# Earlier x loads in the prefix stages, and buffers of their own for two weight quarters in the second main super-tile

## The reference

```
xn  = layernorm(x)
q, k = xn @ Wq, xn @ Wk            # 1024 each, 4 heads of 256
v, gate = xn @ Wv, silu(xn @ Wg)   # 2048 each, 4 heads of 512
g   = log_sigmoid(xn @ Wgk1 @ Wgk2 + b) / 16
attn = gated linear attention over chunks, with a state S per head:
       S <- S * exp(sum g) + k^T v;  o = q S + masked (q k^T) v, rms-normed, * gate, @ Wo
ffn = top-2 of 4 experts, each  ln(relu(ln(xn @ W1 + b1)) @ W2 + b2), weighted
out = x + attn + ffn
```

## Time and profile before

| | us |
|---|---|
| timed runs, lowest, median, highest of 3 | 2788.45, 2792.22, 2792.83 |
| profiled execution, its own time | 2793.73 |
| its span, core 7 (slowest) | 2792.2 |
| its span, core 5 (fastest) | 2761.0 |
| busy on core 7: TensorE, VectorE, ScalarE | 1547.4, 951.5, 881.1 |

### The profile page before, as it was taken

How to read it: one execution, slowest core, us unless ns; L and a number is a source line. 1 busy time by engine, 2 the same in 40 slices (tenths; PEclk the granted TensorE clock), 3 DMA queues, 4 the chain that set the end, 5 groups by cost and what they waited for, 6 DMA issues and landing times.

```text
span 2792.2 us, 25322 instructions; the slowest of 8 cores (2761.0 to 2792.2 us)
## 1 busy us (share of the span) xinstructions
PE 1547.4 (55%) x6272; PEld 584.9 (21%) x6272; DVE 951.5 (34%) x2139; ACT 881.1 (32%) x1617; POOL 107.0 (4%) x152
## 2 busy tenths in 40 slices
PE   1390529235589055648766661289345656966850
PEld 0140104101234021213222220134112212322310
DVE  2432433243401233242255252520233322253253
ACT  2410632044223223214543433303322222533531
POOL 1000000000000000000010000000000000000000
PEclk9695769666799578768888875699767877988975
DMA  8022432162153300117363553035411004635323
GB/s 125 0 31 45 61 46 31 27 95 32 15 76 61 60 16 17 22 19 112 66 109 65 87 81 120 0 44 80 76 21 23 15 16 68 99 65 86 57 35 120
DMA packets 258284, 155.31 MB, mean 56 GB/s; under 512 B 173016, under 2 KB 242648, under 8 KB 258144
## 3 DMA queue, kind: packets, MB, share of 16 engines
q0 software_dynamic: 84576, 94.96, 22.5%
q1 hardware_dynamic: 168960, 41.96, 8.5%
q10 hardware_dynamic: 4608, 16.78, 1.8%
HBM read 198.04 MB, written 8.39 MB: 74 GB/s over the span
## 4 chain that ended last, share of the span: by engine, by line
PE 49%; DVE 19%; DMA 12%; issue 8%; ACT 7%; DVEq 2%; SPq 1%; ACTq 0%; POOL 0%; POOLq 0%
PE pa L287 20%; PE pb L287 19%; PE pf L287 7%; DVE s_bb L540 4%; DMA s_kgT<-s_kgs 4%; DVE s_kgs L653 2%; DMA s_gx<-x_tm 2%; DMA s_ogf<-s_ogc 2%; ACT s_sg L466 2%; DVEq L64 2%; PE pc L287 1%; PE pd L287 1%; DVE s_z L911 1%; DVE s_z L917 1%; DMA s_xt<-xp_tm 1%
## 5 line engine op out<-in xcount | busy, mean ns | idle before, releaser
L287 PE MATMUL pa<-s_w,s_xn 128*128 128x512 bf16 x1280 | 331.4, 406 | 350.7 <-DVE s_v L627 187.8
L287 PE MATMUL pb<-s_w,s_xn 128*128 128x512 bf16 x1280 | 310.0, 386 | 4.1 <-DMA s_w<-W 4.1
L287 PEld LDWEIGHTS pa<-s_w,s_xn 128*128 128x128 bf16 x1280 | 124.9, 102 | 521.9 <-issue 401.8
L287 PE MATMUL pf<-s_w,s_ogf 128*128 128x512 bf16 x512 | 150.7, 467 | 123.4 <-DMA s_ogf<-s_ogc 123.4
L287 PE MATMUL pa<-s_w,s_hfm 128*128 128x512 bf16 x512 | 128.2, 395 | 74.3 <-DMA s_hfm<-s_h 64.4
L750 ACT ACTIVATE s_jb<-s_ogc 128x512 bf16<-128x512 bf16 x64 | 40.3, 630 | 401.0 <-DVE s_ogc L744 399.0
L287 PEld LDWEIGHTS pb<-s_w,s_xn 128*128 128x128 bf16 x1280 | 122.2, 99 | 163.3 <-issue 33.5
L540 DVE TENSOR_TENSOR_SCAN s_bb<-c_os,s_bb 128x128 f32<-128x128 f32 x256 | 108.8, 425 | 106.1 <-ACT s_bb L533 80.2
L831 DVE TENSOR_TENSOR s_mcol<-s_scol 128x8 f32<-128x8 f32 x16 | 2.7, 167 | 400.9 <-ACT s_jb L891 400.3
L653 DVE TENSOR_SCALAR s_kgs<-s_kd,s_eb 128x128 bf16<-128x128 bf16 x256 | 65.3, 255 | 169.3 <-DMA s_kgT<-s_kgs 110.7
L287 PE MATMUL pb<-s_w,s_hfm 128*128 128x512 bf16 x512 | 122.4, 382 | 0.0
(11 more groups left out here) (176 smaller groups left out, 2278.3 us busy)
## 6 DMA issues: line engine op xcount, KB each, us to landing
s_w<-W POOLq DMA_DIRECT2D x32, 1024.0 KB, 13.5
s_w<-Wv_p POOLq DMA_DIRECT2D x8, 1024.0 KB, 19.2
s_w<-Wv POOLq DMA_DIRECT2D x8, 1024.0 KB, 10.7
s_w<-Wg POOLq DMA_DIRECT2D x8, 1024.0 KB, 17.5
s_w<-Wo POOLq DMA_DIRECT2D x8, 1024.0 KB, 12.0
s_gx<-x_tm ACTq DMA_DIRECT2D x16, 512.0 KB, 4.1
out<-s_jf ACTq DMA_DIRECT2D x16, 512.0 KB, 2.9
s_xt<-xp_tm POOLq DMA_DIRECT2D x4, 1024.0 KB, 10.5
```

The costliest lines, as they stand in the source:

```text
L287: ret = e.matmul(out=o, lhsT=l, rhs=r, start=st, stop=sp)
```

## The change

There are three parts. First, `stage_A_blk` takes two lists of waits in place of one: `load_w` for the x load and `sq_w` for the first Square, which writes `s_xntm`. In the prefix, the load is given no wait but for the x load before it, and the Square waits for all VectorE steps of stage C. The side task passes its list as `load_w`.

Second, two new buffers, `s_w4` at the place of `s_qg` and `s_w5` at that of `s_kd`, 1 MB each. After phase 5 of the first main super-tile's FFN, behind the transposes into `s_xn`, they are loaded with the first quarters of Wv and Wg. The load of `s_w4` waits for all steps of VectorE, ScalarE and TensorE so far; that of `s_w5` for the transposes (`tg`) and TensorE.

Third, the second main super-tile takes no slots for these two quarters; `proj_tm` reads them from the new buffers (`ded`). The slots in the rotation shift by two. The first Silu that writes `s_silu` now also waits for `g_marks`, the end of the output stage before it. The first main super-tile works as before, with slots.

```
...
     s_xntm = alloc("s_xntm", [128, 2, 4, D], BF16, at=offs["s_kd"])
+    s_w4 = alloc("s_w4", [128, NDC, 512], BF16, at=offs["s_qg"])
+    s_w5 = alloc("s_w5", [128, NDC, 512], BF16, at=offs["s_kd"])
...
-    def stage_A_blk(x_src, t0, blk, cpar, ext_w):
+    def stage_A_blk(x_src, t0, blk, cpar, load_w, sq_w=()):
...
-        g_dma(bsl[:, :, :], _rearr(rows), wait=[(gx, gx.n)] + list(ext_w), sem=gx)
+        g_dma(bsl[:, :, :], _rearr(rows), wait=[(gx, gx.n)] + list(load_w), sem=gx)
...
                 wait=[(gx, gw), (gd, cm)] +
-                     (([(tg[par], tg[par].n)] + list(ext_w)) if i == 0 else []))
+                     (([(tg[par], tg[par].n)] + list(sq_w)) if i == 0 else []))
...
-    def proj_tm(dst, Wd, act, vm, pre_slot=None, ev_w=()):
+    def proj_tm(dst, Wd, act, vm, pre_slot=None, ev_w=(), ded=None):
...
-            slot = pre_slot if (q4 == 0 and pre_slot is not None) \
-                else wu_next(Wd[:, q4 * 512:(q4 + 1) * 512])
-            gw = gsl[slot].n
+            if q4 == 0 and ded is not None:
+                wview, gwait = ded
+                slot = None
+            else:
+                slot = pre_slot if (q4 == 0 and pre_slot is not None) \
+                    else wu_next(Wd[:, q4 * 512:(q4 + 1) * 512])
+                wview = slotv(slot, NDC, 512)
+                gwait = (gsl[slot], gsl[slot].n)
...
                     s_op(lambda e, ps=ps, tc=tc, q4=q4: e.activation(
                         out=dst[:, tc, q4 * 512:(q4 + 1) * 512], in_=ps[:, :],
-                        func=act), wait=[(te, te.n)])
+                        func=act), wait=[(te, te.n)] + evw)
+                    evw = []
...
-        demark = [(te, te.n), (ve, ve.n)]
+        sqw = [(ve, ve.n)]
...
-        blks = [stage_A_blk(nsrc, nt0, b, ncp, demark) for b in range(NBLK)]
+        blks = [stage_A_blk(nsrc, nt0, b, ncp, (), sq_w=sqw)
+                for b in range(NBLK)]
...
-        pv = wu_next(Wv[:, 0:512])
-        pg2 = wu_next(Wg[:, 0:512])
+        if wu_pref[0] is not None:
+            dedv = wu_pref[0]
+            wu_pref[0] = None
+            pv = pg2 = None
+        else:
+            dedv = (None, None)
+            pv = wu_next(Wv[:, 0:512])
+            pg2 = wu_next(Wg[:, 0:512])
...
                 elif pi == 5:
                     xnm_n[0] = stage_A_xpose(nA[:NBLK], (te, te.n))
+                    g_dma(s_w4[:, :, :], _rearr(Wv[:, 0:512]),
+                          wait=[(ve, ve.n), (sc, sc.n), (te, te.n)], sem=gs4)
+                    g_dma(s_w5[:, :, :], _rearr(Wg[:, 0:512]),
+                          wait=[(tg[0], tg[0].n), (tg[1], tg[1].n),
+                                (te, te.n)], sem=gs5)
+                    wu_pref[0] = ((s_w4, (gs4, gs4.n)),
+                                  (s_w5, (gs5, gs5.n)))
...
```

More of the change, by code:

```diff
@@ L255, in build @@
     pl = mksem("pl")
+    gs4 = mksem("gs4")
+    gs5 = mksem("gs5")
     xd = mksem("xd")
@@ L407, in stage_A_xpose, with stage_A @@
         return xnm
-    def stage_A(x_src, t0, cpar, ext_w=()):
-        blks = [stage_A_blk(x_src, t0, blk, cpar, ext_w) for blk in range(NBLK)]
+    def stage_A(x_src, t0, cpar):
+        blks = [stage_A_blk(x_src, t0, blk, cpar, ()) for blk in range(NBLK)]
         return stage_A_xpose(blks, None)
@@ L619, in proj_tm @@
                     mm(ps[:, :], s_xn[:, dc, tc * 128:(tc + 1) * 128],
-                       slotv(slot, NDC, 512)[:, dc, :],
+                       wview[:, dc, :],
                        start=(dc == 0), stop=(dc == NDC - 1),
-                       wait=(w0 + [(gsl[slot], gw)] +
+                       wait=(w0 + [gwait] +
                              ([vm] if first else [])) if dc == 0 else [],
@@ L633, in proj_tm, with stage_C @@
                         out=dst[:, tc, q4 * 512:(q4 + 1) * 512], in_=ps[:, :],
-                        func=act), wait=[(te, te.n)])
+                        func=act), wait=[(te, te.n)] + evw)
+                    evw = []
                     rot.done(sc)
-            wu_done(slot)
-    def stage_C(prefix, eq_marks, em_marks, pre=(None, None)):
+            if slot is not None:
+                wu_done(slot)
+    def stage_C(prefix, eq_marks, em_marks, pre=(None, None),
+                ded=(None, None)):
         vm = (te, te.n)
-        proj_tm(s_v, Wv_p if prefix else Wv, None, vm, pre_slot=pre[0])
+        proj_tm(s_v, Wv_p if prefix else Wv, None, vm, pre_slot=pre[0],
+                ded=ded[0])
         if not prefix:
             proj_tm(s_silu, Wg, ACT.Silu, vm, pre_slot=pre[1],
-                    ev_w=g_marks[0])
+                    ev_w=g_marks[0], ded=ded[1])
         qbm = None
@@ L1143, in build @@
         eqm, emm = r_
-        tpms, qbm_, kbm_ = stage_C(False, eqm, emm, pre=(pv, pg2))
+        tpms, qbm_, kbm_ = stage_C(False, eqm, emm, pre=(pv, pg2), ded=dedv)
         if stop == "C" and st >= stop_st:
```

## The result

The changed kernel takes 2763.7 us, the median of 10 runs, against 2791.46 us for the kernel before, also 10 runs. The ratio is 0.9881, with a 95% interval of 0.9849 to 0.9912, so it is 1.2% faster. The prediction said 2764 us, range 2751 to 2778, and faster with a chance of 0.95. Runs in which one die had a lower clock than the other are left out of every ratio here; that is why a ratio can differ a little from the quotient of the medians. By the ratio the change saves 33 us, by the medians 27.8, so its size is known to a few us only. That the median and the forecast agree to 0.3 us is luck: the same kernel, timed once more, has a median of 2757.47 us (experiment 7).

What follows compares the result with a forecast made beforehand. No engine bounds the kernel throughout; each stage has its own bound, so each edit was priced in place. From the profiled 2793.7 us, -27.2 - 12.9 + 7 + 3 = -30.1 gave 2764 us, range 2751 to 2778.

Steps and rivals of the forecast that it cites:

- P: End of both prefix super-tiles: early x loads remove VectorE's waits before its reductions, -27.2 us, ends 0 and 27.6.
- M: Second main super-tile: own buffers remove TensorE's wait for Wg and the slow restart, -12.9 us, ends 11.3 and 12.9.
- F: First main super-tile's FFN: new loads on POOL's queue delay the bc loads and expert 3's apply, +7 us, ends 0 and 16.
- G: Output stage after the first FFN: four weight loads instead of two overlap its first gx loads, +3 us, ends 0 and 6.
- So all of it: Prefix: the whole gain from the closed gaps, 27.2 us, reaches the end, since the diagonal build and state update move along.
- rival 3: Second main super-tile: the stall for Wg only moves to a later weight quarter, M = 0, 2777 us; chance 4%.
- The estimate by the fit of the Trainium skill: First FFN's loads: at 2.0 us plus bytes / 436e3, five loads take 18.8 us and apply is 2 us late.
- The upper end of F: First FFN: transposes as slow as before, last bc landing at 1579.1 + 24.8 = 1603.9, a cost of 16 us.

Runs made afterwards that it cites:

- experiment 7: The changed kernel timed again without an edit, 2757.47 us, and with Wg's second quarter in the second main super-tile loaded later, 2758.64 us.
- e1: The changed kernel without the two new buffers' loads, keeping only the early x loads in the prefix: 0.993 of the kernel before, 2771.8 us.
- e4: e3 with the same two buffers also loaded for the first main super-tile: 0.9847 of the kernel before, 2746.07 us.
- e8: The changed kernel without an edit, timed again: 0.9906 of the kernel before, 2757.47 us.
- e2: The changed kernel with the old prefix waits put back, keeping only the two new buffers: 0.9985 of the kernel before, 2785.36 us.
- e3: The changed kernel with the loads of s_w4 and s_w5 one phase later, behind W2[3] and the bc loads: 0.991 of the kernel before, 2762.52 us.
- e5: The changed kernel with one more unused 1 MB load on POOL's queue right behind that of s_w5: 0.9919 of the kernel before, 2766.56 us.
- e9: The changed kernel with Wg's second quarter in the second main super-tile held back, three loads before the output stage: 0.9888 of the kernel before, 2758.64 us.

## Why the prediction was right, step by step

**The whole.** Forecast -30.1 us from the profiled execution of the slowest core, measured -27.8 by the medians of the runs and -27.6 by the sum of the stages over the cores. The mechanism of each term was found as told. The sizes were less good: P and M gave 3.9 us less than forecast and F and G cost 6.2 us less (G by the output stage, below), and 4.6 us were lost in stages that the forecast does not mention. These errors cancel, so the sum came out closer than its parts, and that is luck.

**P was right in kind, and oversized for the median core.** Forecast 27.2, measured 24.3. The loads are issued at 156.66 us (forecast 155.2) and the gaps vanish to the 0.1 us that the prediction left. On core 7 alone the term holds (the first prefix super-tile takes 334.7 us against 349.7), but core 7 was the core with the largest gaps. The idle time before the reductions at the two places sums to 27.6 us on core 7 and to 21.3 to 26.0 on the others, with medians of 12.1 and 11.5 over the cores, since the first x load took 11.9 us to land on core 7 and 9.1 to 11.7 on the others. All of it reached the end of its super-tile: TensorE's first wait shrank by 13.95 us on core 1 and 14.33 on core 7, and e1 has 23.3 us in the prefix by itself. Not all of it reached the end of the kernel: e1 as a whole is 19 us faster by time and 14.1 by its stages, see "What was left out". The prediction's "So all of it" holds for the prefix only.

**M was right.** Forecast 12.9, ends 11.3 and 12.9. The column has 10.1 in the changed kernel, with G inside it. Cut at VectorE's last wait for a gx load, the part up to the first Wo load takes 224.4 us before and 225.1 in e1, and 212.5 in the changed kernel, 211.9 to 212.6 in all kernels with the buffers. So M is 11.9 us, and the slow restart is in it: over the cores of the kernel before, the wait is 9.0 to 11.4 us, mean 10.1, and where it is short the restart is long. On core 6 two groups of eight matmuls are slow, where core 7 has one:

```profile
1869.04 3.57 PE L287 MATMUL pa<-s_w,s_xn 128*128 128x512 bf16 x8 [9.01 <-DMA s_w<-Wg]
1872.40 3.08 PE L287 MATMUL pb<-s_w,s_xn 128*128 128x512 bf16 x8
```

Against 1.89 us for a group at full clock that is 2.9 us, and wait and restart together are 11.4 to 12.9 us on all cores. e4 has the same in the other main super-tile, 13.6 us. In the projections of the second main super-tile the changed profile has no wait of TensorE for a later weight quarter, so rival 3 is out; the one short wait there is for the Silu, and it is no new one: TensorE's list has it twice in the kernel before too, 1.1 us together, and 1.2 here:

```profile
1835.59 1.89 PE L291 MATMUL pa<-s_w,s_xn 128*128 128x512 bf16 x8 [0.66 <-ACT s_silu L641]
```

**F had the right mechanism and was mis-sized.** Forecast +7, measured 3.4 on VectorE and 2.2 in the stage; on core 1, 2.6. Mis-sized were two durations of the working, both too long: the transposes took 16.68 us, and with what lay around it the load of `s_w5` left 19.1 us after they began, where 22 was said; from there to the last landing took 22.5 us, where 24.3 was said. The estimate by the fit of the Trainium skill (DMA: Bandwidth & Descriptors, Anatomy of one DMA), 2 us, was nearer, but not by its rule: the trace has 22.5 us for the loads where the fit, applied to the five of them as one, has 18.8, so it does not agree. F was 4.6 us too large on core 1; the transposes make about 2.9 of that and the loads 1.8. The upper end of F adds 24.8 where the working has 24.3; the 16 us stand either way.

**G was small.** Forecast +3, measured 0.6 to 1.7 by the waits; the output stage itself, from the issue of the Wgk loads to VectorE's last wait for a gx load, takes 74.0 us before, 75.6 in the changed kernel and 74.3 in e8. As a mean over the cores the first two gx loads took 4.87 and 4.70 us, where they took 4.04 and 4.17 before; the other six took 4.1 to 4.4 in both. Loss at half the rate over the whole overlap was too much; only the first two loads meet the weights.

**What was left out.** The attention part of the second main super-tile is +3.1 us in the changed kernel. It is not the buffers: e1, which leaves that super-tile as it was, has +2.8, e2, which has them, +1.3, and e3, e4, e5, e8 and e9 +3.5 to +3.8. It goes with the early x loads. The mean granted clock of this part over the eight cores is 0.772 before and 0.771 in e2 (343.1 and 344.4 us), and 0.764 to 0.768 in the seven executions with early x loads and one `s_kgs` (changed, e1, e3, e4, e5, e8, e9: 345.9 to 346.9 us). The attention part of the first main super-tile has 343.4 us before and 342.6 in e2, and 344.0 to 348.2 in those seven. So part of what P gains in the prefix seems to be lost again where TensorE gets a lower clock; the prediction put nothing there, and there is one execution of each kernel to go by. In the kernel before, the same 544 weight loads of its attention stage took 292.0 us on core 2 and 302.6 us on core 7. By windows (engines, then granted clock):

```profile
1998.20:2290.20 292.00, 139.16 (x533) 51.19 (x544) 96.94 (x256) 66.70 (x146) 0.00 (x1) 0.77 0.11 21
...
2000.80:2303.40 302.60, 150.37 (x544) 53.39 (x544) 96.95 (x256) 66.71 (x146) 0.00 (x0) 0.74 0.10 20
```

VectorE and ScalarE are busy for the same time to 0.01 us; TensorE for 11 us more, of which about 3 are the 11 matmul records missing on core 2, at a granted clock of 0.74 against 0.77. So a stage that the change doesn't touch can differ by 10 us between cores. Whether the earlier x loads cause the lower clock, and how, stays open.

## What to carry to other kernels

Price a gap on all cores and not on the slowest one: here the slowest core also had the largest gaps, 27.6 us against 21.3 to 26.0, and the program gained what the typical core did. A load that waits in a queue shared with others costs what is queued behind it, and its place in the queue cures that wait at no cost in memory, though here the gain in the kernel's time was too small to measure. And before closing a gap, look at what fills the rest of the same stage: a second buffer in a chain of write and transpose gave 84 us here, the earlier loads next to it 24.

## What the runs showed of the hardware

One more load of 1 MB in bf16 (2 MB read as float32) ahead of others on the queue delayed them by 6.7 us. The eight transposes out of `s_xntm` took 24.7 to 28.9 us with 2.5 MB of loads beside them and 16.1 to 19.6 us with one 1 MB load beside them, on all cores of the eleven profiled executions. The granted TensorE clock over one and the same stage differed between cores of one execution by 0.03, and the core with the lower one took 10.6 us of 300 longer.
